# The two rests of a message in a smoothing pass, divided between VectorE and GpSimd

## The reference, cut to what matters

```python
hh = x
for _ in range(3):
    lx = x - segment_sum(w[:, None] * x[src], dst, num_segments=n)
    y = x - gamma * 2.0 * (1.0 - LAMBDA_AMP) * lx
    x = hh + proximal_l21(y - hh, gamma * LAMBDA_AMP)
```

## Time and profile before

| | us |
|---|---|
| median of 3 runs | 8149.56 |
| lowest and highest run | 8144.39, 8155.41 |
| the profiled execution's own time | 8145.88 |
| its span | 8144.0 |

### The profile page before, as it was taken

How to read it: one execution, slowest core, us unless ns; L and a number is a source line. 1 busy time by engine, 2 the same in 40 slices (tenths; PEclk the granted TensorE clock), 3 DMA queues, 4 the chain that set the end, 5 groups by cost and what they waited for, 6 DMA issues and landing times. The chain is left out here.

```text
span 8144.0 us, 280276 instructions
## 1 busy us (share of the span) xinstructions
PE 6943.6 (85%) x98699; PEld 5906.3 (73%) x98724; DVE 5918.6 (73%) x17405; ACT 4418.0 (54%) x13288; POOL 2861.5 (35%) x2957
## 2 busy tenths in 40 slices
PE   0289999999999989999996588788896899998887
PEld 0155555555555579999996588788896888897877
DVE  1266666666666679899896799799899666676556
ACT  0222222222222269999996587687796565665545
POOL 0068888888888855455454000000000000000000
PEclk9999999999999999999998799999998999998889
DMA  9222232222322247767665688787895666664545
GB/s 383 113 55 61 59 61 59 60 59 60 60 60 61 59 157 231 230 227 230 226 228 174 231 300 292 276 298 283 291 332 205 201 197 197 197 192 137 171 134 157
DMA packets 656410, 1425.57 MB, mean 175 GB/s; under 512 B 284336, under 2 KB 351662, under 8 KB 652737
## 3 DMA queue, kind: packets, MB, share of 16 engines
q1 hardware_dynamic: 538370, 1220.03, 46.6%
q0 software_dynamic: 101792, 92.82, 5.5%
q10 hardware_dynamic: 15700, 105.61, 3.2%
HBM read 982.95 MB, written 433.34 MB: 174 GB/s over the span
## 5 line engine op out<-in xcount | busy, mean ns | idle before, releaser
L243 POOL DMA_INDIRECT sorted_rows<-sort_rows,sort_row_at x1600 | 1975.2, 1234 | 518.0 <-issue 496.4
L1560 ACT ACTIVATE smooth_msg<-smooth_ps_a,smooth_w_rows 128x64 f32<-128x64 f32 x6000 | 1311.6, 333 | 313.3 <-PE smooth_ps_a L1646 297.1
L273 ACT ACTIVATE sort_count<-sort_ps_c 50x50 bf16<-50x50 f32 x1600 | 331.9, 207 | 1983.8 <-PE sort_ps_c L305 1348.2
L1341 ACT ACTIVATE poly_cast<-poly_mat 128x1536 bf16<-128x1536 uint8 x500 | 714.2, 1475 | 462.3 <-PE poly_ps L1362 362.8
L301 PEld LDWEIGHTS sort_ps_r<-sort_count,sort_hot_dt 50*125 50x125 bf16 x1600 | 283.3, 177 | 836.5 <-issue 639.1
L315 PE MATMUL sort_ps_m<-sort_w,sort_hidden 128*125 128x64 f32 x3200 | 879.3, 430 | 0.0
L1668 PE MATMUL smooth_ps_s<-smooth_msg,smooth_hot 128*128 128x64 bf16 x7500 | 769.1, 194 | 76.8 <-DVE smooth_last_part L1799 67.0
L294 PE MATMUL sort_ps_h<-sort_attrs,sort_w 24*128 24x500 f32 x800 | 812.6, 1117 | 2.5 <-DMA sort_attrs<-in_attr_t 2.5
L1668 PE MATMUL smooth_ps_s<-smooth_last_part,smooth_hot 128*128 128x64 bf16 x7500 | 763.6, 194 | 15.9 <-issue 15.9
L1668 PE MATMUL smooth_ps_s<-smooth_rest,smooth_hot 128*128 128x64 bf16 x7500 | 764.7, 194 | 14.3 <-issue 14.3
L1668 PEld LDWEIGHTS smooth_ps_s<-smooth_msg,smooth_hot 128*128 128x128 bf16 x7500 | 685.8, 99 | 111.9 <-DVE smooth_last_part L1799 68.9
(11 more groups left out here) (332 smaller groups left out, 16487.0 us busy)
## 6 DMA issues: line engine op xcount, KB each, us to landing
poly_mat<-counts_t SPq DMA_DIRECT2D x500, 400.0 KB
smooth_src<-src_rows SPq DMA_DIRECT2D x150, 960.0 KB, 5.0
smooth_hot<-hot_rows SPq DMA_DIRECT2D x150, 960.0 KB, 6.9
smooth_src<-src_rows SPq DMA_DIRECT2D x150, 640.0 KB, 6.0
smooth_hot<-hot_rows SPq DMA_DIRECT2D x150, 640.0 KB, 6.3
sorted_rows<-zeros ACTq DMA_DIRECT2D x100, 875.0 KB, 13.3
graph_edges<-sorted_rows SPq DMA_DIRECT2D x125, 700.0 KB
hot_rows<-graph_hot SPq DMA_DIRECT2D x125, 640.0 KB, 3.4
```

The source lines that it names most:

```text
L243: pool.indirect_dma_start(out=sorted_rows, out_offset=bass.IndirectOffsetOnAxis(row_at[u][:, j:j + 1], 0), in_=rows[u][:, j, :], in_offset ...
L1341: act.activation(cast[u][h][:, DVE_S:HR, :], mat[u][h][:, DVE_S:HR, :], ACT.Copy)\
L1560: last = act.activation(at[:, i, :], ps_a[g % 2][:, i * D:(i + 1) * D], ACT.Copy, scale=w_rows[u][:, c * CHUNK + i:c * CHUNK + i + 1])
```

## The change

A constant is new, `BY_POOL = 3`. In every pass, from pair 4 on, GpSimd makes both rests of the first three of a chunk's ten blocks (192 columns), and VectorE those of the other seven (448 columns). Pairs 0 to 3 of a pass are as they were. GpSimd waits for ScalarE's part of the chunk (`scaled_a`), makes the first rest, waits for it, and makes the second, which raises `pool_rests`; it goes chunk by chunk in the order of VectorE. TensorE's `add_up` waits for `pool_rests` as well as for `rests`, for chunks from pair 4 on. Since pair 4 adds up chunks of pair 3, for which there is nothing to wait for from GpSimd, TensorE's pair 4 now stands as straight code ahead of a loop that begins with pair 5.

```diff
@@ -1120,6 +1120,8 @@
 
 BY_ACT = 8
 
+BY_POOL = 3
+
 LOADS = ((0, 20), (20, 50))
 
 
@@ -1502,7 +1504,7 @@
             sem(n) for n in ("looked_a", "looked_v", "scaled_a", "scaled_v", "w_kept", "firsts", "rests"))
         chunk_done, sums_kept = sem("chunk_done"), sem("sums_kept")
         step, normed, rooted, posted, taken = (sem(n) for n in ("step", "normed", "rooted", "posted", "taken"))
-        first = sem("first")
+        first, pool_firsts, pool_rests = sem("first"), sem("pool_firsts"), sem("pool_rests")
         row_of = lambda k, p, u: k * NB + u + 2 * p
         part_of = lambda b: (0, b) if b < LOADS[0][1] else (1, b - LOADS[1][0])
         STEPS, LAST_STEPS = 14, 9
@@ -1539,12 +1541,30 @@
             @blk.gpsimd
             def _(pool):
                 n = spilled.count(pool)
+
+                def split(k, p, u, c):
+
+                    own = N_CHUNKS * (k * (NB - 2 * LATE) + u - 2 * LATE) + 2 * N_CHUNKS * p + c
+                    blocks = slice(0, BY_POOL)
+                    pool.wait_ge(scaled_a, N_CHUNKS * row_of(k, p, u) + c + 1)
+                    pool.sem_inc(taken, 1)
+                    pool.tensor_tensor(rest[c][:, blocks, :], msg[c][:, blocks, :], high(msg[c])[:, blocks, :],
+                                       ALU.subtract).then_inc(pool_firsts, 1)
+                    pool.wait_ge(pool_firsts, own + 1)
+                    pool.sem_inc(taken, 1)
+                    pool.tensor_tensor(last_part[c][:, blocks, :], rest[c][:, blocks, :], high(rest[c])[:, blocks, :],
+                                       ALU.subtract).then_inc(pool_rests, 1)
+
                 spilled.clear(pool, True)
                 for k in range(PASSES):
                     spilled.on_pool(pool, k, n, y_sb)
                     pool.wait_ge(spilled.y_in, 16 * k + 16)
                     if k < PASSES - 1:
                         spilled.clear(pool, False)
+                    with pool.Fori(LATE, PAIRS) as p:
+                        for u in two:
+                            for c in range(N_CHUNKS):
+                                split(k, p, u, c)
 
             @blk.scalar
             def _(act):
@@ -1654,6 +1674,8 @@
                     if c * CHUNK in (LOADS[0][0], LOADS[1][0]):
                         pe.wait_ge(hot_in[u][part_of(c * CHUNK)[0]], 16 * PAIRS * k + 16 * p + 16)
                     pe.wait_ge(rests, number + 1)
+                    if not isinstance(p, int) or p >= LATE:
+                        pe.wait_ge(pool_rests, number + 1 - N_CHUNKS * 2 * LATE * (k + 1))
                     if c == 0 and not (isinstance(row, int) and row < 2):
                         pe.wait_ge(sums_kept, row - 1)
                     if c == 0:
@@ -1688,7 +1710,9 @@
                         pair(k, p)
                         if p == SPILL_AT:
                             spilled.on_tensor(pe, k, n)
-                    with pe.Fori(LATE, PAIRS) as p:
+
+                    pair(k, LATE)
+                    with pe.Fori(LATE + 1, PAIRS) as p:
                         pair(k, p)
                 for c in range(N_CHUNKS - ADD, N_CHUNKS):
                     add_up(PASSES - 1, PAIRS - 1, 1, c)
@@ -1786,7 +1810,9 @@
                                 beside.held = False
                             dve.wait_ge(scaled_a, number + 1)
                             dve.wait_ge(scaled_v, number + 1)
-                            dve.tensor_tensor(rest[c][:], msg[c][:], high(msg[c]), ALU.subtract).then_inc(firsts, 1)
+                            blocks = slice(0 if isinstance(p, int) and p < LATE else BY_POOL, CHUNK)
+                            dve.tensor_tensor(rest[c][:, blocks, :], msg[c][:, blocks, :], high(msg[c])[:, blocks, :],
+                                              ALU.subtract).then_inc(firsts, 1)
                             if c + 1 < N_CHUNKS or u == 0:
                                 scale(k, p, u + (c + 1) // N_CHUNKS, (c + 1) % N_CHUNKS)
                             elif not isinstance(p, int) or p < PAIRS - 1:
@@ -1796,8 +1822,8 @@
                                 scale(k + 1, 0, 0, 0)
                             beside.go(at_once)
                             dve.wait_ge(firsts, number + 1)
-                            dve.tensor_tensor(last_part[c][:], rest[c][:], high(rest[c]), ALU.subtract)\
-                               .then_inc(rests, 1)
+                            dve.tensor_tensor(last_part[c][:, blocks, :], rest[c][:, blocks, :],
+                                              high(rest[c])[:, blocks, :], ALU.subtract).then_inc(rests, 1)
                             beside.go(at_once)
                             if c == 0 and u == 0:
                                 ahead.end()
```

## The result

The changed kernel takes 8171.1 us (median of 10 runs, 8166.86 to 8183.88), against 8149.36 us for the kernel before (10 runs). The ratio is 1.0028, 95% interval [1.0019, 1.0038]. The forecast was 8142, so it had the wrong sign; the time lies inside the stated range. The profiled execution took 8168.16 us with a span of 8166.5.

What follows compares the result with a forecast made beforehand. VectorE was taken to bound the loops. Pairs 6 to 21 gave -23.2 us, the last three -4.4, cold code +20.5, together -7.1, so 8142 us was forecast, range 8045 to 8268.

Steps and rivals of the forecast that it cites:

- What bounds the loop: Smoothing's loop pairs: VectorE sets the pace at 21.87, 21.88 and 19.68 us; TensorE's own floor is 18.5 us a pair.
- What VectorE saves: VectorE's rests: 192 columns less save 0.203 us a rest, 4.05 us a pair over 20 rests.
- The length of a turn: GpSimd's subtraction of 192 columns at the shared ports: 0.49 us, of which VectorE is held for 0.36.
- What covers a turn: VectorE's gaps, product and one-operand steps hide part of each hold; turns cost 3.45 us a pair, 3.80 in pass 3.
- The cold code: TensorE's pairs 4 and 5: straight code and the loop's first turn both run cold, +20.5 us, bounds 0 and 25.
- The sum: Whole kernel: -23.2 for pairs 6 to 21, -4.4 for the last three, +20.5 for cold code, together -7.1 us.
- C: Rival, VectorE's rests: GpSimd comes between two bare rests each time, 5.80 us a pair, +120, 8270 us; chance 0.17.
- D: Rival, shared ports: a turn holds VectorE for GpSimd's whole record, 0.13 us more, +118, 8268 us; chance 0.08.
- E: Rival, shared ports: no contention, so TensorE is next at 18.5 us a pair, -144, 8006 us; chance 0.08.
- F: Rival, loop pairs: GpSimd becomes the last one at 19.2 us a pair, TensorE waits for `pool_rests`, 8180 us; chance 0.12.

Runs made afterwards that it cites:

- the kernel with seven blocks: Against the kernel before: VectorE makes seven blocks' rests from pair 4 on, nobody the other three; GpSimd idle there, work left out; 7959.43 us, ratio 0.9763.

## Why the prediction was wrong, step by step

**What bounds the loop: right.** VectorE did, and behind it TensorE, at 18.01 us a pair where the estimate was 18.5.

**What VectorE saves: right.** 4.05 us a pair: the rests of the kernel with seven blocks have a mean of 0.62 us, 0.20 less than before, and that kernel falls to TensorE's bound.

**The length of a turn: right.** 0.50 us where 0.49 was taken from three bounds, VectorE held for 0.36 to 0.37, released 0.14 before the record ends where the earlier trace rows had shown 0.13. The records of 1.00 us are the 0.96 of the prediction.

**What covers a turn: this step failed.** The prediction said that a turn costs "0 behind the product and a one-operand step", and let one-operand steps behind a second rest cover one too. Two kinds of such steps do not cover but are held themselves. The groups of pairs 6 to 21 of pass 1, mean of one in ns behind the busy time:

```profile
L1799 DVE TENSOR_TENSOR smooth_msg<-smooth_ps_v,smooth_w_rows 128x128 f32<-128x128 f32 x160 | 45.0, 281 | 0.0
...
L1777 DVE TENSOR_SCALAR xs<-smooth_z,dinv 125x64 f32 x32 | 10.6, 371 | 0.0
...
L1762 DVE TENSOR_SCALAR smooth_norm<-smooth_norm 125x2 f32<-125x2 f32 x16 | 7.5, 471 | 0.0
...
L1785 DVE CAST sums_rest<-smooth_left 125x128 f32 x16 | 7.3, 454 | 0.0
L1760 DVE TENSOR_SCALAR smooth_shrink<-smooth_norm 125x2 f32<-125x2 f32 x16 | 7.1, 444 | 0.0
...
L1756 DVE TENSOR_REDUCE smooth_norm<-smooth_sq 125x2 f32<-125x128 f32 x16 | 4.4, 277 | 0.0
...
L1764 DVE RECIPROCAL smooth_norm<-smooth_norm 125x2 f32<-125x2 f32 x16 | 2.5, 155 | 0.0
```

In the kernel before the same lines, in the same order, had 284, 248, 162, 217, 160, 277 and 155 ns. The tensor-scalar steps and one cast are longer by 2 x 0.123 + 0.309 + 0.237 + 0.284 = 1.08 us a pair; the sum had 0.09 for these places. The reduction, the reciprocal and the product are not touched.

It is GpSimd's subtractions that hold them, and not the narrower rests around them: in the kernel with seven blocks, where GpSimd does nothing, the same steps are as short as before. Two of its groups:

```profile
L1754 DVE TENSOR_SCALAR smooth_norm<-smooth_norm 125x2 f32<-125x2 f32 x16 | 2.6, 162 | 0.0
L1752 DVE TENSOR_SCALAR smooth_shrink<-smooth_norm 125x2 f32<-125x2 f32 x16 | 2.5, 157 | 0.0
```

The other cast (`sums_rest<-xs`, 0.210 us) is not held in the changed kernel. That is a matter of who comes first: with five blocks on GpSimd it is held, and the cast that is held here is not:

```profile
L1780 DVE CAST sums_rest<-xs x16 | 8.7, 544 | 0.0
...
L1784 DVE CAST sums_rest<-smooth_left 125x128 f32 x16 | 3.5, 218 | 0.0
```

Turns cost 22.18 - 21.87 + 4.05 = 4.36 us a pair in passes 1 and 2, where 3.45 were forecast. The lengthened records of VectorE account for nearly all of it in pass 1, against the same lines of the kernels before and with seven blocks: 1.80 us in the rests, 1.39 in the steps with two operands, 1.08 in the tensor-scalar steps and the cast. So the term that the sum had at 0.09 came out 0.99 larger, and the whole miss is 0.91; the rest of the sum was close, in total. In pass 3, which has only the two small tensor-scalar steps, these are longer by 0.60 us, and turns cost 4.02 against 3.80, so there the other places cost 0.4 less than forecast.

The Trainium skill has these kinds in "SBUF — State Buffer", section "Who interferes with whom": copies, casts and tensor-scalar operations can use the shared pair of ports, and a reduction never contends; the trace agrees with both. The prediction drew on that section for the hold and passed over this part of it. What no run isolates is what the pair would gain if these steps were of a kind that is not held; a turn that is not met there might be met at the next rest.

**The cold code: the term was mis-sized.** 20.5 us were forecast, for pairs 4 and 5. In the changed kernel these are +4.0 us together, in the kernel with the straight pair alone +6.7, and that kernel as a whole is 10 us over the one before by its runs.

**The sum.** Pairs 6 to 21: -23.2 forecast, +5.1 + 4.8 - 0.4 = +9.5 measured. The last three pairs, where "more steps give more cover": -4.4 forecast, about +1.5 measured, nearly all of it in pass 3. Pairs 0 to 5: +20.5 forecast, +10.9 in the profile, of which 6.9 are in pairs 0 to 3, where the change does nothing and single profiles differ by as much. Together -7.1 against some +22. The error in the turns, 39 us with the last pairs, was partly hidden by the 10 us too much for pairs 0 to 5. That is luck: by the forecast's own cold code the kernel would have come out some 10 us slower still.

**The rivals.** C named the point of decision, 0.203 us a turn net: the turns cost 0.22 in passes 1 and 2 and 0.20 in pass 3. Its own mechanism, GpSimd between two bare rests each time, is not what the rows show. It would have cost 5.80 us a pair, 1.4 more than measured, and turns do meet the product, as at 4799.02, and leave it as it is. D fell with the release 0.14 us before the record's end. E fell, and is what the kernel whose GpSimd only writes shows, some 180 us under the kernel before. F is not the cause either: in pairs 6 to 21 of pass 1 TensorE waits for GpSimd's line 12 times, 12.3 us in all, at the head of a row, where before it waited 16.0 us for VectorE's; and VectorE has no more idle time than before.

## What to carry to other kernels

Work moved from VectorE to GpSimd paid here only while a turn cost VectorE less, net, than the moved columns saved. So compare the hold (here 0.04 us and 0.00166 a column) with what VectorE saves (0.00105 a column) and with its gaps (0.27 around a product out of PSUM, 0.07 between two subtractions), and not the two engines' busy times. Try smaller sizes: 128 columns gained 0.6% where 192 lost 0.2%. Before a VectorE instruction is counted as cover, look at its kind: here reductions, reciprocals and products out of PSUM were never held in any of the kernels, and tensor-scalar operations and casts were, whenever GpSimd's subtraction had started first.

## What the runs showed of the hardware

- GpSimd's subtraction of float32 and a bfloat16 half read in place: 0.18 us and 0.00166 us a column, from four sizes.
- Writing alone on GpSimd (0.258 us for 192 columns) leaves VectorE's subtractions at 0.62 us, but a tensor-scalar operation of VectorE beside it has a mean of 0.306 us where it had 0.248.
- GpSimd's wait for its own instruction before costs 0.18 us each time, 114.0 us over 630 chunks.
- Neither engine has precedence in the rows read: the one that came second was let in when the other had read its columns (VectorE 0.37 us after GpSimd's start at 192 columns, GpSimd 0.48 us after VectorE's start at 448).
- VectorE is let in 0.14 us before GpSimd's record ends, at 64, 128, 192 and 320 columns alike.
